# Attention over channels on one core: TensorE's order around the Gram block, VectorE's order of reading T, and the place of element 2's Gram block

## The chip, the core and the metric

The kernel runs on one core of one Trainium2 chip. The metric is the device time in microseconds (us) of one execution. Five engines work beside each other, each through its own list of instructions in order, and wait for each other on semaphores: TensorE (PE) multiplies into the eight PSUM banks, VectorE (DVE) and ScalarE (ACT) read these banks, GpSimd (POOL) works in SBUF alone, and SyncE (SP) issues transfers. TensorE's clock has two levels, 1.2 and 2.4 GHz; the profile gives it as a share of the higher one.

## The reference

Input x has shape (8, 256, 32, 16): batch element b, position s, channel c, and m. For each element:

```python
xn = groupnorm(x, G=8)                      # groups of 2 of the 16 m; over s and c
Q, K, V = (einsum('oc,bscm->bsom', W, xn) + bias for W, bias in (q, k, v))   # 256 outputs each
A = softmax(Q' @ K', axis=-1)               # per (b, m): 256 x 256, summed over s
out = einsum('bmcC,bmsC->bsCm', A, V')
y = x + einsum('oc,bscm->bsom', Wo, out) + bo
```

All is float32.

## The kernel before, in words

The kernel never forms Q and K. For an element and an m it needs only the 32x32 Gram matrix of the centred x (`xc`), its column sums, and the group's variance. T = (normalised Gram) x Wk plus bias terms is a 32x256 matrix for each m, and the scores Q'K' are Wq times T. The 16 m of an element are 4 groups of 4: `t` counts 0 to 3 and `q` the four partition quarters. The work of an element is pipelined over the elements around it, and each element is 16 slots, `s`. In every slot each of three engines does one piece of the scores: PE one 99x512 matmul into one of four score banks (`score`, L449), which is 3 slots ahead; DVE its row maxima (`maximum`, L693), 2 slots ahead; ACT the exponentials with their row sums, two instructions of 256 columns (`exponentials`, L942). `score(n)` waits until ACT has done exponentials n-4.

Between these, every engine has pieces of other elements at fixed slots. The orders are written out by hand: the tables `PE_AT`, `DVE_AT`, `ACT_AT` (L42 to L46) give the slot of each piece for elements 1 to 7, the bodies of `element` in the PE block (L535) and in the DVE block (L746) hold a list of their own for element 0 and the order inside a slot.

The pieces, for an element j of which element b = j-3 or j-2 is in its slots:

- `sum_rows(j)`, `sum_groups(j)`, `mean(j)`, `read_mean(j)`: group means (PE, DVE, PE, DVE); POOL then centres the rows (`centre_rows`, L1008).
- `gram_of(j)` (L379, 64 small matmuls) and `sums_of(j)` (L389, 64 more) write the Gram matrices and column sums; `read_gram(j)` (DVE L659) copies them; POOL takes the diagonal (`diagonal`, L1016); `sum_diagonal(j)` (DVE L663), `variance(j)` (PE L405) and `read_variance(j)` (DVE L668, L675) give the variances.
- POOL's `deviations(j)` (L1030, L1050, L1056) makes the scaled sums `ssum` and `sblk`, and `normalise(j)` (L1024) the scaled Gram `gnorm`.
- `t_product(j)` (PE L431) writes T in four banks: t=0 into `acc` (its upper half), t=1 into `bx`, t=2 into `by`, t=3 into `bz`; `tb_product(j)` (L437) writes the bias rows into `bz`. DVE reads them with `read_t(j, t)` (L682) and `read_tb(j)` (L688). POOL splits T in a high and a low part (`parts`, L1082 and L1084), and SP's transfers stack them for the score matmuls.
- `column_sums(b, g)` (PE L473, 16 matmuls of 256 columns, g = 0 to 3) sums the exponentials, weighted with the inverse row sums (`invert`, DVE L704), into the lower half of `acc`; `read_acc`, `a_columns` (L489), `read_a`, POOL's `scale_wo` (L1095, L1099), `weights` (L507, L515), `read_weights` (DVE L728, L730) make the output weights; `y_half` (PE L531) makes half of y, and ACT (`read_y01`, L954) or DVE (`read_y23`, L741) reads it. From element 2 on ACT reads y01 of element b-2 behind the exponentials of slot 0.

The bank `bx` carries sums, means, Gram matrices and variances of the elements from 2 on, and T's part t=1. So `gram_of(j)` waits until DVE has read t=1 of element j-1 (`pe.wait_ge(t_done, 4 * (j - 1) + 2)`, L375; for j = 2 the wait isn't there, because that block runs before T of element 1 is written). `t_done` counts reads of T in DVE's order. In elements 1 to 4 PE's slot 10 is `score`, `gram_of(b+3)`, `column_sums(b, 0)`; DVE's slot 8 is `maximum`, `read_t(., 0)`, its slot 9 `maximum`, `read_tb`, `read_t(., 1)`.

Before element 0 PE runs `score(0)`, `score(1)`, `gram_of(2)`, `sums_of(2)`, `score(2)` (L629 to L633), and DVE `centre(2)`, `maximum(1)`, `diagonal_first(2)`, `read_gram(2)`, `sum_diagonal(2)` (L902 to L906). `t_product(1)` in slot 0 of element 0 waits for `gram_done` 3, that is for `read_gram(2)`.

## Time and profile before

| | us |
|---|---|
| runs of the kernel before | 188.49, 189.87, 194.72 (median 189.87) |
| the profiled execution | 190.13 |
| its span in the profile | 188.1 |
| busy in the span: PE, DVE, ACT, POOL | 161.7, 133.0, 130.2, 96.9 |

The profile covers the span; 2.0 us of the execution lie around it. Times in rows are counted from the span's start. The first exponentials of an element (slot 0) start at 23.8 us for element 0, 50.6 for element 1, 68.1 for element 2 and 86.8 for element 3. Ends of matmuls are modelled, so that two neighbouring ones seem to overlap a little. A figure in square brackets behind a row is the idle time of the engine before it, and what ended it.

### The profile page before, as it was taken

Reading aid. Unit: us, or ns where it says so; the run is one execution under the profiler, and the core shown is the slowest. Engines: PE = TensorE matmul, PEld = TensorE weight load, DVE = VectorE, ACT = ScalarE, POOL = GpSimd, SP = SyncE. Lnnn points to the kernel's source line nnn. Section 1 sums busy time; section 2 is a strip of 40 time slices with the busy share of each in tenths; the row PEclk is TensorE's granted clock in tenths of the full one; section 3 lists DMA queues with packets and bytes.
Section 4 is the critical chain, followed back from the end, with each engine's and each line's share of the span. In section 5 each row is a group of like instructions: output and inputs, shape, how many; then the busy total and the mean of one; then the engine's idle time right before and its main releaser. Section 6 shows DMA issues by size and latency. Waiting matters only on the chain.

```text
span 188.1 us, 6983 instructions
## 1 busy us (share of the span) xinstructions
PE 161.7 (86%) x2672; PEld 93.6 (50%) x2672; DVE 133.0 (71%) x327; ACT 130.2 (69%) x533; POOL 96.9 (52%) x155
## 2 busy tenths in 40 slices
PE   7986969979799799979997899798989879999872
PEld 7765845524344464446444644463435435344541
DVE  4349359857469887888788777877898684678531
ACT  2001045975378969996998689968999999499721
POOL 1561385985386757675767476757274050007300
PEclk9999765555869999999999999999999995899996
DMA  6613974289289629962883297518935790002032
GB/s 220 179 37 72 228 213 179 39 191 236 112 162 196 213 30 205 226 233 36 186 202 151 29 200 154 201 24 202 227 124 82 195 265 35 0 0 115 2 137 89
DMA packets 10286, 26.46 MB, mean 141 GB/s; under 512 B 2731, under 2 KB 3726, under 8 KB 10254
## 3 DMA queue, kind: packets, MB, share of 16 engines
q1 hardware_dynamic: 8512, 25.16, 52.4%
q10 hardware_dynamic: 1742, 0.87, 1.8%
q8 instruction: 21, 0.34, 0.8%
q14 instruction: 11, 0.09, 0.1%
HBM read 8.85 MB, written 4.19 MB: 69 GB/s over the span
## 4 chain that ended last, share of the span: by engine, by line
PE 54%; ACT 14%; DVE 8%; issue 6%; POOL 3%; DVEq 0%; POOLq 0%
PE s_bank L449 15%; PE acc L473 14%; ACT e_sb L942 11%; PE bz L531 7%; ACT yb L954 3%; PE acc L431 3%; PE bx L379 3%; PE bx L389 2%; PE bz L437 2%; PE by L507 2%; DVE negmax L693 2%; PE bx L405 2%; DVE t_sb L682 1%; DVE t_sb L688 1%; PE by L515 1%
## 5 line engine op out<-in xcount | busy, mean ns | idle before, releaser
L942 ACT ACTIVATE e_sb<-s_bank,negmax 128x256 f32<-128x256 f32 x256 | 117.5, 494 | 25.0 <-DVE negmax L693 24.8
L693 DVE TENSOR_REDUCE negmax<-s_bank 128x2 f32<-128x512 f32 x128 | 84.8, 678 | 13.6 <-PE s_bank L449 13.1
L449 PE MATMUL s_bank<-stack,wq_st 99*128 99x512 f32 x128 | 56.8, 505 | 5.5 <-ACT e_sb L942 5.4
L942 ACT ACTIVATION_READ_ACCUMULATOR e_sb<-s_bank,negmax 128x1 f32 x256 | 57.8, 226 | 0.0
L449 PEld LDWEIGHTS s_bank<-stack,wq_st 99*128 99x128 f32 x128 | 23.3, 208 | 31.8 <-issue 31.5
L473 PE MATMUL acc<-e_sb,recip 128*32 128x256 f32 x512 | 37.6, 415 | 0.6 <-DVE recip L704 0.6
L1095 POOL TENSOR_TENSOR aR<-aT,coef 128x32 f32<-128x32 f32 (+1 forms) x16 | 3.6, 247 | 36.3 <-DVE aT L717 36.3
L1084 POOL TENSOR_TENSOR t_parts<-t_sb,t_parts 128x768 fp32r<-128x768 f32 (+1 forms) x14 | 21.7, 1552 | 1.1
L473 PEld LDWEIGHTS acc<-e_sb,recip 128*32 128x32 f32 x512 | 14.4, 115 | 15.0 <-issue 8.8
L1008 POOL TENSOR_TENSOR xc<-xs,nm 128x512 f32<-128x512 f32 x13 | 13.8, 1080 | 10.1 <-DVE nm L653 10.1
L954 ACT ACTIVATE yb<-bz,beff 128x256 f32<-128x256 f32 x16 | 6.7, 470 | 14.6 <-PE bz L531 14.6
L1030 POOL TENSOR_TENSOR rs_all<-vare,power 128x8 f32<-128x8 f32 x8 | 13.2, 1644 | 4.7 <-DVE vare L668 4.5
L531 PE MATMUL bz<-xT,wf 32*32 32x256 f32 x224 | 15.0, 382 | 0.1
L1099 POOL TENSOR_TENSOR ws<-wo_sb,aR 128x1024 f32<-128x1024 f32 (+1 forms) x8 | 14.4, 1803 | 0.6
L1082 POOL CAST t_parts<-t_sb 128x768 fp32r<-128x768 f32 (+1 forms) x14 | 10.1, 718 | 8.0 <-DVE t_sb L682 8.0
L346 PE MATMUL bz<-idle 128*128 128x128 f32 x60 | 11.3, 351 | 1.0 <-POOL idle L1110 1.0
L379 PE MATMUL bx<-xc 128*32 128x32 f32 x448 | 5.9, 210 | 6.3 <-DVE t_sb L682 4.2
L346 PEld LDWEIGHTS bz<-idle 128*128 128x128 f32 x60 | 9.9, 253 | 2.2 <-issue 1.2
L379 PEld LDWEIGHTS bx<-xc 128*32 128x32 f32 x448 | 5.3, 123 | 8.4 <-issue 8.4
L531 PEld LDWEIGHTS bz<-xT,wf 32*32 32x32 f32 x224 | 5.7, 105 | 6.0 <-issue 2.0
L431 PE MATMUL acc<-wk_sb,gnorm 32*128 32x256 f32 x14 | 5.7, 494 | 3.4 <-issue 2.2
L1016 POOL TENSOR_TENSOR gdiag<-gram,k_sb 128x128 f32<-128x128 f32 x6 | 2.7, 457 | 11.0 <-DVE gram L659 11.0
(119 smaller groups left out, 199.2 us busy)
## 6 DMA issues: line engine op xcount, KB each, us to landing
stack<-t_parts SPq DMA_DIRECT2D x28, 256.0 KB, 5.0
stack<-t_parts SPq DMA_DIRECT2D x36, 128.0 KB, 5.0
xs<-x_rows SPq DMA_DIRECT2D x8, 512.0 KB, 4.9
xT<-x_cols SPq DMA_DIRECT2D x8, 512.0 KB, 5.6
y_cols<-yb SPq DMA_DIRECT2D x7, 512.0 KB, 5.2
stack<-t_parts SPq DMA_DIRECT2D x8, 32.0 KB
stack<-t_parts ACTq DMA_DIRECT2D x4, 64.0 KB, 3.5
stack<-t_parts SPq DMA_DIRECT2D x4, 64.0 KB, 2.7
```

The costliest lines, as they stand in the source:

```text
L346: nc.tensor.matmul(bz[:, 0:P], idle[:, :], idle[:, :], start=True, stop=True)
L379: mm = nc.tensor.matmul(stat_bank(j)[C * q:C * q + C, C * t:C * t + C], xc[:, j % 2, ch, Q * t + q, 0:C], xc[:, j % 2, ch, Q * t + q, 0:C] ...
L449: nc.tensor.matmul(s_bank[q][:, :], wq_st[:, P * h:P * h + P], stack[:, b % 2, q, 2 * tt:2 * tt + 2, :].rearrange("p t n -> p (t n)"), sta ...
L473: mm = nc.tensor.matmul(acc[C * q:C * q + C, 0:CH], recip[:, at:at + C], e_sb[:, 4 * g + q, i, :], start=(g in opens and i == 0), stop=(g ...
L531: mm = nc.tensor.matmul(dst[C * q:C * q + C, S * i:S * i + S], wf[C * q:C * q + C, t, :], xT[C * q:C * q + C, j, t, :], start=True, stop=True)
L693: nc.vector.tensor_reduce(negmax[:, n % NS, :], s_bank[n % NS][:, :].rearrange("p (i n) -> p i n", i=2), op=ALU.max, axis=AX.X, negate=Tru ...
L942: last = nc.scalar.activation(e_sb[:, s, i, :], s_bank[q][:, CH * i:CH * i + CH], ACT.Exp, bias=negmax[:, q, i:i + 1], accum_out=rowsum[:, ...
L954: last = nc.scalar.activation(yb[:, yb_of(j), t, :], src[:, S * i:S * i + S], ACT.Identity, bias=beff[:, t:t + 1])
L1008: last = nc.gpsimd.tensor_tensor(xc[:, j % 2, ch, :, 0:C].rearrange("p (g k) c -> p g k c", g=G), xs[:, j % XS, ch, :, :].rearrange("p (g ...
L1030: nc.gpsimd.tensor_tensor(rs_all[:, :], vare[:, j, 0:8], power[:, :], ALU.pow).then_inc(rs_all_done, 1)
L1084: nc.gpsimd.tensor_tensor(t_parts[:, j % 2, 1, rows, :], t_sb[:, rows, :], t_parts[:, j % 2, 0, rows, :].bitcast(f32), ALU.subtract).then_ ...
L1099: nc.gpsimd.tensor_tensor(ws[:, :, ms, :], wo_sb[:, :, None, :].to_broadcast([P, HC, n, C]), aR[:, :, 0, ms, None].to_broadcast([P, HC, n, ...
```

## The change

On PE, `column_sums(b, 0)` goes ahead of `gram_of(b + 3)` in slot 10 of elements 1 to 4. On DVE, `read_t(b + 2, 1)` goes from slot 9 to slot 8, ahead of `maximum` and `read_tb` of slot 9; in element 0 it goes ahead of `read_tb` too. `gram_of(2)` and `sums_of(2)` go from before `score(2)` to slots 2 and 3 of element 0, and their reads on DVE to slots 3 and 4; `gram_of(2)` gets the wait for t=1 of element 1, and `t_product(1)` waits for the mean of element 2 in place of its Gram. Everything that follows in element 0 moves to later slots (variance of 2 from slot 3 to 5, T of 2 from 9 to 10, `gram_of(3)` from 12 to 13, `sums_of(3)` from 13 to 14; DVE's `read_gram(3)` from 13 to 15), and `variance(3)` and what is tied to it goes into element 1, whose `sum_rows(4)` and `mean(4)` move one slot. The instructions are the same ones, and so is the number of each. The half of y that DVE reads (`read_y23`) is not touched by the diff.

```diff
--- before.py
+++ after.py
@@ -41,7 +41,7 @@
 
 PE_AT = dict(sums2=1, rows=1, mean=3, sums3=3, y23=4, a=5, t=7, gram=10, sums0=10, gsums=12, weights=13, sums1=13,
              variance=15, y01=15)
-DVE_AT = dict(variance=0, invert3=1, groups=2, mean=4, acc=4, y23=5, invert0=6, a=6, t0=8, tb=9, t1=9, t2=10, t3=11,
+DVE_AT = dict(variance=0, invert3=1, groups=2, mean=4, acc=4, y23=5, invert0=6, a=6, t0=8, t1=8, tb=9, t2=10, t3=11,
               invert1=11, gram=13, weights=14, invert2=13, trace=14)
 ACT_AT = dict(y01=0)
 
@@ -370,7 +370,7 @@
                 pe.wait_ge(centred, j + 1)
                 if j == 0:
                     pe.wait_ge(centred_by_dve, 1)
-                if j >= 3:
+                if j >= 2:
 
                     pe.wait_ge(t_done, 4 * (j - 1) + 2)
                 for t in range(T):
@@ -397,9 +397,6 @@
                 pe.wait_ge(trace_done, j + 1)
                 if j == 0:
                     pe.wait_ge(set_blocks, 2)
-                if j == 2:
-
-                    pe.wait_ge(t_done, 4 + 2)
 
                 for k in range(2):
                     mm = nc.tensor.matmul(stat_bank(j)[:, T * k:T * (k + 1)], half_m[:, k, :], trace[:, :],
@@ -417,7 +414,7 @@
                 pe.wait_ge(gnorm_done, j + 1)
                 if j == 1:
 
-                    pe.wait_ge(gram_done, 3)
+                    pe.wait_ge(mean_done, 3)
                     pe.wait_ge(tb_done, 1)
                 elif j >= 2:
 
@@ -542,30 +539,36 @@
                         if s == 0:
                             t_product(1)
                             tb_product(1)
+                        if s == 2:
+                            gram_of(2)
                         if s == 3:
+                            sums_of(2)
+                        if s == 5:
                             variance(2)
-                        if s == 5:
+                        if s == 7:
                             sum_rows(3)
-                        if s == 7:
+                        if s == 8:
                             mean(3)
-                        if s == 9:
+                        if s == 10:
                             t_product(2)
                             tb_product(2)
-                        if s == 11:
+                        if s == 12:
                             column_sums(0, 0)
-                        if s == 12:
+                        if s == 13:
                             gram_of(3)
-                        if s == 13:
+                        if s == 14:
                             column_sums(0, 1)
                             sums_of(3)
-                        if s == 15:
-                            variance(3)
                         continue
+
+                    late = 1 if b == 1 else 0
+                    if b == 1 and s == 1:
+                        variance(3)
                     if s == PE_AT["sums2"]:
                         column_sums(b - 1, 2)
-                    if b + 3 < B and s == PE_AT["rows"]:
+                    if b + 3 < B and s == PE_AT["rows"] + late:
                         sum_rows(b + 3)
-                    if b + 3 < B and s == PE_AT["mean"]:
+                    if b + 3 < B and s == PE_AT["mean"] + late:
                         mean(b + 3)
                     if s == PE_AT["sums3"]:
                         column_sums(b - 1, 3)
@@ -576,10 +579,10 @@
                     if b + 2 < B and s == PE_AT["t"]:
                         t_product(b + 2)
                         tb_product(b + 2)
+                    if s == (6 if last else PE_AT["sums0"]):
+                        column_sums(b, 0)
                     if b + 3 < B and s == PE_AT["gram"]:
                         gram_of(b + 3)
-                    if s == (6 if last else PE_AT["sums0"]):
-                        column_sums(b, 0)
                     if b + 3 < B and s == PE_AT["gsums"]:
                         sums_of(b + 3)
                     if s == (9 if last else PE_AT["sums1"]):
@@ -628,8 +631,6 @@
             pe.wait_ge(t_done, 4)
             score(0)
             score(1)
-            gram_of(2)
-            sums_of(2)
             score(2)
             for b in range(B):
                 element(b)
@@ -753,43 +754,47 @@
                         if s == 0:
                             read_t(1, 0)
                         if s == 1:
+                            read_t(1, 1)
                             read_tb(1)
-                            read_t(1, 1)
                         if s == 2:
                             read_t(1, 2)
                         if s == 3:
                             read_t(1, 3)
+                            diagonal_first(2)
                         if s == 4:
+                            read_gram(2)
+                            sum_diagonal(2)
+                        if s == 6:
                             read_variance(2)
-                        if s == 6:
+                        if s == 7:
                             sum_groups(3)
-                        if s == 7:
+                        if s == 9:
                             read_mean(3)
-                        if s == 9:
                             invert(0, 0)
-                        if s == 10:
+                        if s == 11:
                             read_t(2, 0)
-                            read_tb(2)
-                        if s == 11:
                             read_t(2, 1)
                         if s == 12:
-                            read_t(2, 2)
+                            read_tb(2)
                             invert(0, 1)
                         if s == 13:
+                            read_t(2, 2)
+                        if s == 14:
                             read_t(2, 3)
-                            read_gram(3)
-                        if s == 14:
                             invert(0, 2)
                         if s == 15:
-                            sum_diagonal(3)
+                            read_gram(3)
                         continue
-                    if b + 2 < B and s == DVE_AT["variance"]:
+                    late = 1 if b == 1 else 0
+                    if b == 1 and s == 0:
+                        sum_diagonal(3)
+                    if b + 2 < B and s == DVE_AT["variance"] + late:
                         read_variance(b + 2)
                     if s == DVE_AT["invert3"]:
                         invert(b - 1, 3)
-                    if b + 3 < B and s == DVE_AT["groups"]:
+                    if b + 3 < B and s == DVE_AT["groups"] + late:
                         sum_groups(b + 3)
-                    if b + 3 < B and s == DVE_AT["mean"]:
+                    if b + 3 < B and s == DVE_AT["mean"] + late:
                         read_mean(b + 3)
                     if s == DVE_AT["acc"]:
                         read_acc(b - 1)
@@ -802,10 +807,10 @@
                     if b + 2 < B:
                         if s == DVE_AT["t0"]:
                             read_t(b + 2, 0)
+                        if s == DVE_AT["t1"]:
+                            read_t(b + 2, 1)
                         if s == DVE_AT["tb"]:
                             read_tb(b + 2)
-                        if s == DVE_AT["t1"]:
-                            read_t(b + 2, 1)
                         if s == DVE_AT["t2"]:
                             read_t(b + 2, 2)
                         if s == DVE_AT["t3"]:
@@ -901,9 +906,6 @@
             dve.wait_ge(xs_loaded[2], 16)
             centre(2, (0, 1), centred)
             maximum(1)
-            diagonal_first(2)
-            read_gram(2)
-            sum_diagonal(2)
             dve.wait_ge(w_loaded, 16 * 4)
             nc.vector.tensor_reduce(wv_sum[:, :], wv_sb[:, :, :], op=ALU.add, axis=AX.X).then_inc(wv_sum_done, 1)
             for b in range(B):
```

## Rows read from the trace of the kernel before

**Rows 1.** The longest waits over the span, and PE's at the Gram block (us, times, longest).

```profile
ACT e_sb L942 <- DVE negmax L693: 24.8, 22, 8.3
...
ACT yb L954 <- PE bz L531: 14.6, 8, 2.7
...
PE bx L379 <- DVE t_sb L682: 4.2, 4, 1.1
```

**Rows 2.** The page: TensorE's granted clock in 40 slices, and the chain by engine.

```profile
PEclk9999765555869999999999999999999995899996
...
PE 54%; ACT 14%; DVE 8%; issue 6%; POOL 3%; DVEq 0%; POOLq 0%
```

**Rows 3.** Windows of elements 1, 2 and 5: busy us of each engine, clock, DMA.

```profile
50.60:68.07 17.47, 15.14 (x255) 8.36 (x259) 14.30 (x35) 15.19 (x64) 13.09 (x20) 0.90 0.66 154
68.07:86.75 18.68, 16.66 (x328) 9.55 (x321) 15.37 (x37) 15.87 (x68) 12.69 (x20) 1.00 0.72 175
...
124.50:141.00 16.50, 14.31 (x174) 7.23 (x170) 13.24 (x32) 14.27 (x61) 9.84 (x16) 1.00 0.68 164
```

**Rows 4.** Timeline of element 2, slots 8 to 11 (start us, us, engine, line, operation).

```profile
79.64 0.47 DVE L682 SCALAR_TENSOR_TENSOR t_sb<-bk_sb,ssum,acc 128x256 f32<-128x256 f32 x1
...
79.93 1.02 PE L449 MATMUL s_bank<-stack,wq_st 99*128 99x512 f32 x3
...
80.47 0.69 DVE L693 TENSOR_REDUCE negmax<-s_bank 128x2 f32<-128x512 f32 x1 [0.36 <-PE s_bank L449]
...
81.08 0.46 DVE L688 SCALAR_TENSOR_TENSOR t_sb<-bk_sb,rows_all,bz 32x256 f32<-32x256 f32 x1
...
81.47 0.46 DVE L682 SCALAR_TENSOR_TENSOR t_sb<-bk_sb,ssum,bx 128x256 f32<-128x256 f32 x1
...
82.07 0.75 PE L379 MATMUL bx<-xc 128*32 128x32 f32 x64 [1.13 <-DVE t_sb L682]
...
82.68 1.07 PE L473 MATMUL acc<-e_sb,recip 128*32 128x256 f32 x16
```

**Rows 5.** Timeline of element 2, its end: weights read, y01 read.

```profile
87.25 0.29 DVE L728 TENSOR_TENSOR wf<-by,k_sb 128x128 f32<-128x128 f32 x1 [0.88 <-PE by L515]
...
89.66 0.84 ACT L954 ACTIVATE yb<-bz,beff 128x256 f32<-128x256 f32 x2 [1.87 <-PE bz L531]
```

**Rows 6.** Timeline of element 5, which has no Gram block.

```profile
137.39 1.07 PE L473 MATMUL acc<-e_sb,recip 128*32 128x256 f32 x16
...
139.07 0.47 ACT L942 ACTIVATE e_sb<-s_bank,negmax 128x256 f32<-128x256 f32 x1 [0.35 <-DVE negmax L693]
...
140.24 0.47 PE L449 MATMUL s_bank<-stack,wq_st 99*128 99x512 f32 x1 [0.90 <-ACT e_sb L942]
```

**Rows 7.** Timeline of the start: Gram block of element 2, T of element 1.

```profile
25.27 1.08 PE L379 MATMUL bx<-xc 128*32 128x32 f32 x64 [1.97 <-DVE xc L834]
...
26.11 1.04 PE L389 MATMUL bx<-xc 128*32 128x1 f32 x64
...
28.08 0.24 POOL L1056 TENSOR_TENSOR sblk<-ssum,k_sb 128x32 f32<-128x32 f32 x1
...
29.70 1.06 PE L437 MATMUL bz<-wk_sb,sblk 128*32 128x256 f32 x2
...
30.69 1.65 PE L449 MATMUL s_bank<-stack,wq_st 99*128 99x512 f32 x3
```

**Rows 8.** Timeline of element 0 from its slot 9 on.

```profile
39.72 0.79 PE L431 MATMUL acc<-wk_sb,gnorm 32*128 32x256 f32 x1 [1.22 <-POOL gnorm L1024]
...
43.03 1.94 PE L473 MATMUL acc<-e_sb,recip 128*32 128x256 f32 x16
...
49.68 0.30 DVE L659 COPY gram<-bx 128x132 f32<-128x132 f32 x1 [2.88 <-PE bx L389]
...
50.61 0.47 ACT L942 ACTIVATE e_sb<-s_bank,negmax 128x256 f32<-128x256 f32 x1 [3.14 <-DVE negmax L693]
...
51.58 0.58 PE L405 MATMUL bx<-trace,half_m 128*128 128x4 f32 x4 [1.30 <-DVE trace L663]
```

## The prediction, made before the changed kernel was built or run

> **What bounds the kernel now.** I read the waits first. ACT is idle for 24.8 us behind DVE's maxima and for 14.6 us behind the y01 matmuls, and PE is idle for 4.2 us, in 4 pieces of up to 1.1 us, ahead of a Gram block, each time until DVE has read a piece of T [rows 1]. An idle engine costs only if the end hangs on it, so the chain comes next: 54% of it is PE, 14% ACT, 8% DVE [rows 2]. Then the windows: in element 2 (18.68 us) PE is busy for 16.66 us, ACT for 15.87, DVE for 15.37, POOL for 12.69; element 5, which has no Gram block, takes 16.50 [rows 3]. So no engine is full, and PE's order of work sets the pace. The loop closes at y01: PE comes to the end of its slots, y01 follows, ACT has waited for it (1.87 us in element 2) and only then does the next exponentials, which PE's next scores need [rows 5]. Whatever PE's order saves between two y01 is saved in full, as long as DVE and ACT keep up.
>
> **The steady part, elements 1 to 4.** In element 2, PE's three scores of slots 8 to 10 end at 79.93 + 1.02 = 80.95. Then it waits 1.13 us for T's part t=1, whose read begins at 81.47, behind a maximum (80.47) and the bias rows (81.08); the Gram block starts at 82.07, the column sums of group 0 at 82.68, and these take 1.07 us [rows 4]. After the change, the column sums start at 80.95. What they wait for is there: T's part in acc was read from 79.64 on, and the inverse row sums are of slot 6. They end near 82.0. DVE reads t=1 straight behind t=0, from 80.05 to 80.5, in the 0.36 us which it sat idle ahead of the maximum [rows 4]. That maximum slips by at most 0.05 us, as the score it reads ends at about 80.45. So the Gram block finds its bank free and starts near 82.0, and the slot-11 scores start about 1.0 us earlier. Each half of this edit alone would hide nearly all of the wait; the two don't add up.
>
> Can the others follow? DVE's bias rows stay at 81.1 and the maximum of slot 10 comes 0.4 us earlier, since t=1 no longer stands ahead of it. From there to the copy of the Gram matrices DVE has little idle time, so it is 0.3 to 0.4 us earlier there and not 1.0. But it then waits for the weight matmuls anyway, 0.88 us ahead of the copy at 87.25 [rows 5]; with PE 1.0 us earlier and DVE 0.35 us earlier that wait is 0.2 us, and y01 still gains nearly the whole. For ACT: the exponentials of slot 12 start 0.35 us earlier and then run back to back, 0.9 us a slot, so that the last score that PE issues in the element (slot 15) needs exponentials that are done about a microsecond before it. POOL gets the bias rows and t=1 0.4 us earlier. What stands behind the moved column sums on PE is the Gram block alone, and it isn't later than before. The sum for elements 1 to 4 is the wait that goes, 4.2 us [rows 1], less 0.05 us each: 4.0 us. Its bounds are 1.0 us (the wait returns as one for ACT, rival C) and 4.4.
>
> **Element 5** has the new order on DVE but no Gram block. There PE waits 0.90 us for ACT at 140.24, because the exponentials of slot 12 began at 139.07, 0.35 us after ACT ran out, behind the bias rows, t=1 and a maximum [rows 6]. With t=1 moved into an idle gap that maximum is 0.4 us earlier: 0.35 us saved, bounds 0 and 0.5. Elements 6 and 7 read no T, so nothing changes there.
>
> **Element 0 and the seam to element 1.** This is the part that I know least. The steps, with PE at its lower clock:
>
> - Before, PE did the Gram block and sums of element 2 from 25.27 to 27.15, ahead of score 2. T of element 1 stood behind them and the copy of the Gram, its bias rows started at 29.70, the next scores at 30.69; POOL's sblk, which the bias rows need, ended at 28.08 + 0.24 = 28.3 [rows 7]. After, T doesn't wait for the Gram copy and runs near 24.3, but the bias rows still wait for POOL until 28.4. So the scores start at 29.4 in place of 30.69: 1.3 us gained, not 4, and the idle time of PE grows, which before held 1.9 us of Gram and sums.
> - These two blocks now stand in slots 2 and 3: 1.08 us [rows 7] and about 0.85, minus 1.9 us. Behind them DVE's diagonal waits for the sums until about 33.4, with a maximum queued behind it: ACT gets its seventh exponentials (slot 6) at about 34.4, as before. PE then waits about 0.9 us for the trace ahead of variance 2: minus 0.9 us.
> - Before, PE waited 1.22 us at 39.72 for POOL's gnorm of element 2 [rows 8]. POOL has that ready at 39.7 again: it splits T of element 1 about 1.5 us earlier but then waits for the later variance. PE arrives at about 40.6, so the wait is used up: plus 1.2 us.
> - Before, ACT lost 3.14 us at 50.61, because DVE stood 2.88 us in the copy of Gram 3 at 49.68, with two maxima behind it, and PE lost 1.30 us at 51.58 to the trace of element 3 [rows 8]. With the copy in slot 15 behind two more maxima and variance 3 in the next element, both mostly go: plus 1.3 us on PE.
>
> The sum is 1.3 - 1.9 - 0.9 + 1.2 + 1.3 = 1.0 us. Moving rows and mean of element 4 by a slot I cost at nothing: centring it took place well ahead of the Gram block, and POOL idles. By ACT alone the gain would be more (3.14 us less some 1.5 that comes back two slots later). I take 1.2 us, nearer PE's sum since PE is the chain. The bounds: minus 2.0 (the 1.9 us of added blocks with nothing regained) and plus 3.0 (ACT's wait gone whole).
>
> **The sum.** 4.0 + 0.35 + 1.2 = 5.55 us. The profiled execution took 190.13 us (span 188.1 and 2.0 around it), 0.3 above the median of the runs, 189.87. 190.13 - 5.55 = 184.6; against the median it is 184.3. I take 184.8, as two of the three terms were laid out by hand from one execution, and such schedules leave out small waits. A difference of under 2%, 3.8 us, is about what can't be told from none; that border is at 186.1.
>
> **The rivals.**
>
> B, only the steady part pays. Element 0 costs up to 2.0 us instead of giving 1.2: 190.1 - 4.35 + 2.0 = 187.8. For it: 3 us of PE idle time at the start are not filled by anything, and DVE has a new wait at slot 3. Against it: the stalls of 3.14 and 1.30 us at its end are plain in the trace.
>
> C, the wait at the Gram block turns into one for ACT. Element 5 has the coming order already, column sums right behind the scores, and there PE waits 0.90 us for exponentials [rows 6]. If that came back in elements 1 to 4, only 0.2 us each would be left: 190.1 - 0.8 - 0.35 - 1.2 = 187.8; with nothing from the start, 189. Against it: in element 5 neither the Gram block nor the sums stand ahead of that score (0.75 us [rows 4] and about as much), and in elements 1 to 4 they do.
>
> D, slower: the clock. It stands at half in the slices from 28 to 47 us and not fully up until 56 [rows 2]. Element 1 still has 0.90 of it [rows 3]. Full activity near 43 to 50 us, the column sums and Gram 3, came before it rose. After the change PE idles longer at the start and its dense part may come later. If the clock stays at the lower level through element 1, the price is: 4 column sums at 1.94 for 1.07 us, 3.5 [rows 8, 4]; 16 scores, (1.65 - 1.02)/3 = 0.21 each, 3.4 [rows 7, 4]; Gram and sums 0.7; 7.6 us, of which a fifth is paid already: 6.1. With the start's gain lost (1.2) it is 184.8 + 7.3 = 192.1, and with a third of element 2 as well, 194.3. It decides at the first column sums of element 1: if they take 1.9 us and those after them too, it is slower. Against it: the amount of PE work is the same, and the last of element 0 is as dense as it was.
>
> The Trainium skill, "TensorE: Matmul & The Clock Gate", Part 1, says that the throttled state is the default and that activity releases the throttle. It speaks for D, since the change takes activity out of the start; by it the clock could be lower there, where the rows show it at the lower level already, so the trace has nothing for it to take until about 47 us.
>
> E, the same thing the other way: with fewer stalls from 47 us on, the clock doesn't fall again near 52 us. Column sums there, of 1.94 us as the row at 43.03 [rows 8], become 1.07, the sum rows and scores shorter too: 1.5 to 2.5 us more, 182.7.
>
> **How the numbers follow.** The forecast has 0.56, and of it 0.03 above 186.1; E 0.11, B 0.16, C 0.10, D 0.07. Faster by over 2%: 0.53 + 0.11 = 0.64. Within 2%: 0.03 + 0.16 + 0.10 = 0.29. Slower: 0.07. The range has to reach E and B and may leave out D and the end of C: 182.0 to 188.2.
>
> **What would show it.** Right: PE's wait ahead of the Gram block is gone from the waits in elements 1 to 4, the column sums of group 0 follow the scores at once, and the windows from y01 to y01 are about 17.7 us in elements 2 to 4; the first exponentials of element 1 come near 47.5 instead of 50.61 and those of element 2 about 2 us earlier than 68.1. Wrong: a wait of the slot-13 scores for ACT in elements 1 to 4 (C); element 2's first exponentials at 68 us or later (B, D); clock digits of 5 behind 48 us (D). A wait of DVE for sums_of(2) of more than 2 us would also break the sum of element 0.

## The result, and the profile after

The changed kernel took 183.31 us (median of 4 runs, 182.40 to 183.57) against 189.52 for the one before; the ratio is 0.968, 95% interval 0.962 to 0.974. The forecast was 184.8 us, range 182.0 to 188.2. The profiled execution took 182.40 us (span 180.3) against 190.13. Here and below, a ratio with an interval is taken over the runs within 1.5% of the fastest of the same kernel, and a median over all its runs.

The clock in 40 slices and the chain by engine, from the page after; these answer to [rows 2]:

```profile
PEclk9996995555969999999999999999999999999996
...
PE 63%; ACT 21%; issue 6%; DVE 6%; POOL 2%; POOLq 0%; DVEq 0%
```

More of the chain is on PE and ACT than before (63% and 21%, from 54% and 14%). PE does the same 2672 matmuls in both. Its busy time fell from 161.7 to 158.0 us, and its idle time (span less busy) from 26.4 to 22.3: of the 7.8 us of span, 4.1 are waiting that went, and 3.7 are the same matmuls in less time, with 26.7 us at the lower clock in place of 40.3 (how that is worked out stands with the experiments). From the 13th slice to the 39th the digits are all 9s. Before there was a 5 and an 8 about where element 6 ends and element 7 begins, and the window of that stretch in the trace of the kernel before shows what it was (columns as in [rows 3]):

```profile
151.00:162.30 11.30, 10.09 (x106) 5.00 (x106) 7.21 (x17) 8.58 (x39) 2.37 (x3) 0.70 0.38 113
```

A granted clock of 0.70, in a stretch that no edit touches. This has to be kept apart from the change in all that follows.

The waits after, which answer to [rows 1]:

```profile
ACT e_sb L944 <- DVE negmax L694: 17.8, 15, 6.8
...
ACT yb L956 <- PE bz L528: 12.5, 8, 3.2
...
PE bz L434 <- POOL sblk L1058: 2.6, 1, 2.6
```

PE's wait ahead of the Gram block, 4.2 us in 4 pieces, is not among the waits any more. ACT waits 17.8 us for maxima in place of 24.8, and 12.5 for y01 in place of 14.6. There is a new one: 2.6 us for POOL's `sblk`, once, in the start.

Element 2 in the timeline after, where [rows 4] stood before:

```profile
78.24 0.47 DVE L683 SCALAR_TENSOR_TENSOR t_sb<-bk_sb,ssum,acc 128x256 f32<-128x256 f32 x1
...
78.53 1.02 PE L446 MATMUL s_bank<-stack,wq_st 99*128 99x512 f32 x3
...
78.63 0.48 DVE L683 SCALAR_TENSOR_TENSOR t_sb<-bk_sb,ssum,bx 128x256 f32<-128x256 f32 x1
...
79.07 0.69 DVE L694 TENSOR_REDUCE negmax<-s_bank 128x2 f32<-128x512 f32 x1
...
79.47 1.07 PE L470 MATMUL acc<-e_sb,recip 128*32 128x256 f32 x16
...
79.67 0.46 DVE L689 SCALAR_TENSOR_TENSOR t_sb<-bk_sb,rows_all,bz 32x256 f32<-32x256 f32 x1
...
80.36 0.77 PE L379 MATMUL bx<-xc 128*32 128x32 f32 x64
```

The scores end at 79.55. The column sums follow at 79.47 (ends are modelled), the read of t=1 (78.63) stands behind t=0, the Gram block begins at 80.36. From the three scores' start to the Gram block it was 2.14 us and is 1.83, with the column sums already done; those began 2.75 us behind that start before and begin 0.94 behind it now. Windows from the first exponentials of one element to those of the next (elements 1 to 5, answering to [rows 3]):

```profile
46.21:65.32 19.11, 17.25 (x313) 9.31 (x314) 15.00 (x37) 15.33 (x64) 14.52 (x22) 0.91 0.64 148
...
65.32:84.63 19.31, 17.89 (x368) 10.80 (x367) 15.21 (x37) 15.84 (x69) 12.68 (x20) 1.00 0.69 169
84.63:102.43 17.80, 16.56 (x294) 9.58 (x298) 15.20 (x37) 15.84 (x69) 12.67 (x20) 1.00 0.66 153
102.43:120.39 17.96, 17.07 (x359) 10.14 (x348) 15.20 (x37) 15.85 (x69) 12.70 (x20) 1.00 0.64 152
120.39:137.50 17.11, 15.30 (x180) 7.72 (x180) 14.97 (x37) 15.69 (x68) 11.21 (x18) 1.00 0.69 159
```

By these windows elements 1 and 2 are longer than before (19.11 for 17.47 us and 19.31 for 18.68): ACT reaches them earlier and then waits. So the y01 reads, which close the loop, are the better marks. From one to the next it took, before and after: 18.69 and 17.82 us (y01 of element 0 to that of element 1), 19.33 and 17.95, 18.82 and 17.47, 16.32 and 15.92, then 18.13 and 15.82, and 13.15 in both. So the 7.7 us between the two profiled executions are made up of 1.4 us up to the first y01 (70.97 to 69.55), 0.87 + 1.38 + 1.35 = 3.60 in elements 2 to 4, 0.40 in element 5, and 2.31 in element 6, which holds the stretch at a clock of 0.70 that no edit touches.

The start in the timeline after, which answers to [rows 7, 8]:

```profile
24.51 0.50 PE L446 MATMUL s_bank<-stack,wq_st 99*128 99x512 f32 x1 [1.04 <-DMA stack<-t_parts]
...
24.94 0.48 PE L428 MATMUL acc<-wk_sb,gnorm 32*128 32x256 f32 x1
...
28.23 1.06 PE L434 MATMUL bz<-wk_sb,sblk 128*32 128x256 f32 x2 [2.57 <-POOL sblk L1058]
...
34.19 0.47 ACT L944 ACTIVATE e_sb<-s_bank,negmax 128x256 f32<-128x256 f32 x1 [1.41 <-DVE negmax L694]
...
40.31 0.79 PE L428 MATMUL acc<-wk_sb,gnorm 32*128 32x256 f32 x1
...
46.21 0.47 ACT L944 ACTIVATE e_sb<-s_bank,negmax 128x256 f32<-128x256 f32 x1
...
48.51 0.29 PE L389 MATMUL bx<-xc 128*32 128x1 f32 x11 [0.48 <-issue]
...
48.84 0.30 DVE L660 COPY gram<-bx 128x132 f32<-128x132 f32 x1 [1.54 <-PE bx L389]
...
50.00 0.47 ACT L944 ACTIVATE e_sb<-s_bank,negmax 128x256 f32<-128x256 f32 x1 [1.65 <-DVE negmax L694]
...
50.30 0.58 PE L402 MATMUL bx<-trace,half_m 128*128 128x4 f32 x4 [0.60 <-DVE trace L664]
```

PE waits 1.04 us for a transfer of the stack ahead of score 2, which now has no Gram block in front of it. T of element 1 runs at 24.94, then PE waits 2.57 us for `sblk` and does the bias rows at 28.23, 1.5 us earlier than before. The seventh exponentials come at 34.19 after a wait of ACT for DVE, T of element 2 at 40.31 with no wait for `gnorm`. The first exponentials of element 1 are at 46.21 in place of 50.61. DVE's wait of 2.88 us at the copy of Gram 3 is 1.54 now, ACT's of 3.14 at the start of element 1 has become one of 1.65 two slots later (50.00), and PE's trace wait of 1.30 is 0.60. But of 4.4 us at the first exponentials of element 1, 2.75 are left at those of element 2 (65.32 for 68.07) and 1.42 at the first y01:

```profile
65.77 0.41 PE L470 MATMUL acc<-e_sb,recip 128*32 128x256 f32 x3 [1.00 <-issue]
...
69.55 0.84 ACT L956 ACTIVATE yb<-bz,beff 128x256 f32<-128x256 f32 x2 [3.20 <-PE bz L528]
```

Here PE stands for 1.00 us in the middle of column sums, with nothing in the profile that it waits for, and ACT waits 3.20 us for y01. PE's own work shows where the rest went. The sums of element 3 were done at 49.61 before (the first row below) and at 48.80 now, 0.8 us earlier and not 4.4. Up to the first y01 PE does 1036 matmuls in both traces, but of these 307 stood behind the first exponentials of element 1 before, and 389 do now. Its idle time up to the first y01 was 9.66 us and is 8.91. A wait of 0.82 us that went belongs to element 1's own Gram block (the second row) and so to the order and not to the start. From the trace before:

```profile
48.87 0.74 PE L389 MATMUL bx<-xc 128*32 128x1 f32 x64
...
63.40 0.76 PE L379 MATMUL bx<-xc 128*32 128x32 f32 x64 [0.82 <-DVE t_sb L682]
```

### The profile page after: what moved, and what is told of

Read it like the earlier page. It is cut to its first block, busy times and chain, and to the rows that moved or that the text cites. A ratio compares the mean times of both kernels' runs of the same rounds, so it can differ in the third digit from the quotient of the medians.

```text
span 180.3 us, 6983 instructions
## 1 busy us (share of the span) xinstructions
PE 158.0 (88%) x2672; PEld 91.6 (51%) x2672; DVE 132.3 (73%) x327; ACT 130.1 (72%) x533; POOL 96.7 (54%) x155
## 4 chain that ended last, share of the span: by engine, by line
PE 63%; ACT 21%; issue 6%; DVE 6%; POOL 2%; POOLq 0%; DVEq 0%
ACT e_sb L944 17%; PE s_bank L446 16%; PE acc L470 13%; PE bz L528 7%; PE bz L346 4%; ACT yb L956 3%; PE bx L402 2%; PE bx L379 2%; PE bz L434 2%; PE bx L389 2%; PE bx L356 2%; PE acc L428 2%; PE by L504 2%; DVE negmax L694 1%; PE bx L364 1%
## 5 line engine op out<-in xcount | busy, mean ns | idle before, releaser
L944 ACT ACTIVATE e_sb<-s_bank,negmax 128x256 f32<-128x256 f32 x256 | 117.5, 495 | 18.2 <-DVE negmax L694 17.8
L446 PE MATMUL s_bank<-stack,wq_st 99*128 99x512 f32 x128 | 55.8, 491 | 6.5 <-ACT e_sb L944 5.4
L446 PEld LDWEIGHTS s_bank<-stack,wq_st 99*128 99x128 f32 x128 | 22.8, 201 | 31.8 <-issue 29.7
L470 PE MATMUL acc<-e_sb,recip 128*32 128x256 f32 x512 | 35.8, 393 | 1.6 <-issue 1.0
L470 PEld LDWEIGHTS acc<-e_sb,recip 128*32 128x32 f32 x512 | 13.7, 111 | 16.0 <-issue 9.3
L1010 POOL TENSOR_TENSOR xc<-xs,nm 128x512 f32<-128x512 f32 x13 | 13.8, 1080 | 11.3 <-DVE nm L654 11.3
L956 ACT ACTIVATE yb<-bz,beff 128x256 f32<-128x256 f32 x16 | 6.7, 470 | 12.5 <-PE bz L528 12.5
L346 PE MATMUL bz<-idle 128*128 128x128 f32 x60 | 10.8, 337 | 1.0 <-POOL idle L1112 1.0
L346 PEld LDWEIGHTS bz<-idle 128*128 128x128 f32 x60 | 9.3, 237 | 2.6 <-issue 1.6
L434 PE MATMUL bz<-wk_sb,sblk 128*32 128x256 f32 x14 | 5.2, 461 | 2.6 <-POOL sblk L1058 2.6
L710 DVE COPY a_sb<-acc 128x256 f32<-128x256 f32 x9 | 3.8, 425 | 4.2 <-PE acc L470 4.1
L705 DVE RECIPROCAL recip<-rowsum 128x8 f32<-128x8 f32 x32 | 6.2, 194 | 0.9 <-ACT e_sb L944 0.7
L428 PE MATMUL acc<-wk_sb,gnorm 32*128 32x256 f32 x14 | 5.2, 456 | 1.7 <-issue 1.7
```

Of the source, the lines that this page charges most:

```text
L346: nc.tensor.matmul(bz[:, 0:P], idle[:, :], idle[:, :], start=True, stop=True)
L446: nc.tensor.matmul(s_bank[q][:, :], wq_st[:, P * h:P * h + P], stack[:, b % 2, q, 2 * tt:2 * tt + 2, :].rearrange("p t n -> p (t n)"), sta ...
L470: mm = nc.tensor.matmul(acc[C * q:C * q + C, 0:CH], recip[:, at:at + C], e_sb[:, 4 * g + q, i, :], start=(g in opens and i == 0), stop=(g ...
L944: last = nc.scalar.activation(e_sb[:, s, i, :], s_bank[q][:, CH * i:CH * i + CH], ACT.Exp, bias=negmax[:, q, i:i + 1], accum_out=rowsum[:, ...
L956: last = nc.scalar.activation(yb[:, yb_of(j), t, :], src[:, S * i:S * i + S], ACT.Identity, bias=beff[:, t:t + 1])
L1010: last = nc.gpsimd.tensor_tensor(xc[:, j % 2, ch, :, 0:C].rearrange("p (g k) c -> p g k c", g=G), xs[:, j % XS, ch, :, :].rearrange("p (g ...
```

## The experiments

The twelve experiments below time eight kernels, some of them more than once, in three sets beside the kernel before. Times scattered there much more than in the first result: the kernel before took between 186.67 and 201.97 us in 34 runs. Each run also gives its mean granted clock, and most of the scatter goes with it. Time at the lower clock is worked out as 2 x (1 - mean clock) x span, since the lower level is half of the higher one. A least-squares fit over the 107 runs with a known clock, with a constant of its own for each kernel and one slope for all, gives 0.343 us of time (standard error 0.012) for each us at the lower clock, and takes the scatter within a kernel from 3.2 us to 1.0. "At equal clock" means below: by this fit. At 30 us at the lower clock the kernels stand at:

| kernel | runs | us at 30 us of lower clock (standard error) |
|---|---|---|
| before | 35 | 188.3 (0.2) |
| changed | 16 | 183.6 (0.3) |
| PE's order alone | 4 | 185.1 (0.5) |
| DVE's order alone | 4 | 183.6 (0.5) |
| both orders, old start | 18 | 184.0 (0.3) |
| new start, old orders | 6 | 188.1 (0.4) |
| changed, with POOL's edit | 12 | 182.2 (0.3) |
| both orders, old start, with POOL's edit | 6 | 182.7 (0.4) |
| changed, with filler | 6 | 186.1 (0.4) |

How far to trust the table: a constant of its own for each set moves no difference to the kernel before by more than 0.3 us. The fit over the 38 runs within 1.5% of the fastest of their kernel has a slope of 0.27 (error 0.06) and moves these differences by at most 0.5 us, but for the filler kernel, which it puts 0.6 us above the changed one and not 2.4.

The Trainium skill, "TensorE: Matmul & The Clock Gate", Terms, puts the cost of the throttled time at that time multiplied by 1 - K/N, which is 0.5 at half clock. Here it is 0.343, and the measurement decides. The price also differs by place, by two comparisons below: 0.18 in element 0 and 0.37 in element 1.

**pe_only**, on the kernel before:

```diff
+                    if s == (6 if last else PE_AT["sums0"]):
+                        column_sums(b, 0)
                     if b + 3 < B and s == PE_AT["gram"]:
                         gram_of(b + 3)
-                    if s == (6 if last else PE_AT["sums0"]):
-                        column_sums(b, 0)
```

> The kernel before with one edit: column sums of group 0 ahead of the Gram block in slot 10 of elements 1 to 4. Theory (the two orders are two ways around one wait): the column sums, 1.07 us, fill the wait of 1.13 us, so nearly all goes: PE's wait ahead of the Gram block falls from 4.2 us to under 0.5 in total, 4.0 us saved, ratio 0.979. Element 5 gains nothing. Rival (each order gives half): about 2 us, ratio 0.99. Rival (the wait turns into one for ScalarE): under 1 us, and PE's scores wait for the exponentials in slot 13.

Medians of 187.95 us for 194.21, ratio 0.982 (0.942 to 1.021), too wide to say anything by itself; at equal clock 3.2 us less than before. The wait ahead of the Gram block has gone from the list of waits. Element 2 in its timeline:

```profile
83.37 1.07 PE L473 MATMUL acc<-e_sb,recip 128*32 128x256 f32 x16
...
83.96 0.46 DVE L682 SCALAR_TENSOR_TENSOR t_sb<-bk_sb,ssum,bx 128x256 f32<-128x256 f32 x1
...
84.35 0.67 DVE L693 TENSOR_REDUCE negmax<-s_bank 128x2 f32<-128x512 f32 x1
...
84.57 0.75 PE L379 MATMUL bx<-xc 128*32 128x32 f32 x64
```

The column sums end at 84.44 and the read of t=1 at 84.42, so the Gram block starts 0.1 us behind the sums. The y01 reads of elements 2 to 4 lie 18.08, 18.23 and 17.86 us apart, 2.67 us less in sum than before; element 5 gives nothing (16.33 for 16.32). That is the theory, somewhat short in size (about 3.2 of the 4.0 us expected fall to these three elements, by their waits of 1.13, 1.13 and 1.12 us); neither rival.

**dve_only**, on the kernel before:

```diff
-DVE_AT = dict(..., tb=9, t1=9, ...)
+DVE_AT = dict(..., t1=8, tb=9, ...)
+                        if s == DVE_AT["t1"]:
+                            read_t(b + 2, 1)
                         if s == DVE_AT["tb"]:
                             read_tb(b + 2)
-                        if s == DVE_AT["t1"]:
-                            read_t(b + 2, 1)
```

> The kernel before with the other edit alone: VectorE reads t=1 of T behind t=0, ahead of the maximum and the bias rows, in elements 1 to 5. Theory: the read ends before the scores of slot 10 do, so the Gram block starts at once: 4.1 us saved in elements 1 to 4 and 0.35 in element 5, 4.4 in all, ratio 0.977. Rival (each order gives half): 2 us, ratio 0.99.

185.97 us for 194.21, ratio 0.969 (0.940 to 0.999); at equal clock 4.7 us less than before. y01 to y01 17.51, 17.88 and 17.50, so 3.95 us less in three elements, and 15.96 in element 5, 0.36 less. Element 2:

```profile
83.31 0.47 DVE L682 SCALAR_TENSOR_TENSOR t_sb<-bk_sb,ssum,bx 128x256 f32<-128x256 f32 x1
...
84.15 0.76 PE L379 MATMUL bx<-xc 128*32 128x32 f32 x64
...
84.75 0.67 DVE L693 TENSOR_REDUCE negmax<-s_bank 128x2 f32<-128x512 f32 x1
...
84.77 1.07 PE L473 MATMUL acc<-e_sb,recip 128*32 128x256 f32 x16
```

t=1 is read by 83.78, before the scores end at 84.2, and the Gram block follows them at once. The second maximum starts 1.54 us behind the three scores' start (83.21), where in pe_only it starts 1.93 behind it (82.42). This edit alone does all that the two do.

**orders_only**, both of the diffs above.

> The kernel before with both orders and without the move of element 2's Gram block. Theory: the two don't add up, 4.4 us saved, ratio 0.977, within 0.5 us of each alone. Rival (they add up): 8 us, ratio 0.957. What the whole change has over this one is then the worth of the start: the measured ratio is 0.968, so the start would be worth 1.5 to 2 us.

189.60 us for 194.21, with 49.6 us at the lower clock (median of its runs) against 47.3; at equal clock 4.3 us less than before. y01 to y01 17.71, 17.96, 17.47, 15.92. The two orders don't add up: 3.2, 4.7 and 4.3 us for one, the other and both, with errors of 0.5, 0.5 and 0.3 us.

**start_only**, the changed kernel with both diffs above undone.

> The changed kernel with both orders of elements 1 to 5 put back as they were: only the start (Gram block of element 2 in slots 2 and 3, all of element 0 that follows from it, variance 3 in element 1). Theory (the start has a worth of its own, by PE's sum 1.2 us): ratio 0.990 to 0.994, PE waits of 1.1 us ahead of the Gram blocks in elements 1 to 4 are back, first exponentials of element 1 near 46 to 47 us in place of 50.6. Rival (the start only shifts, and the gain beyond 4.4 us came from the clock in the last elements): ratio 0.998 to 1.002, with the first y01 at 71 us as before.

189.83 us for 194.21, ratio 0.985 (0.966 to 1.004). The PE wait ahead of the Gram blocks is back:

```profile
PE bx L379 <- DVE t_sb L683: 4.3, 4, 1.1
```

Its first exponentials of element 1 are 22.9 us behind those of element 0, as in the changed kernel (22.5; before 26.8). But it then took 25.3 us to the first y01, where the kernel before took 20.4, with one stop of PE of 1.33 us and a clock of 0.88 for 0.92. At equal clock it is only 0.2 us (error 0.5) faster than before. Its median time at the lower clock was 32 us against 47 for the kernel before and 50 for the two orders. So a second theory came up: the start pays through the clock. The profiles spoke for it too: with the old start, the clock stayed down through element 1 in all three profiles of this set. Both orders, slices of 4.7 us:

```profile
PEclk9999555556965559999999999999999996999997
```

**after_again** and **orders_again**, the two kernels once more on one chip.

> The changed kernel once more, unchanged, for the time that it spends at TensorE's lower clock. In the traces so far the stretch at the lower clock went on through most of element 1 (from about 50 to 66 us) in three of the four kernels with the old start (not in the profiled execution of the kernel before) and in neither of the two with the new start. Theory (the new start mainly shortens the time at the lower clock): median of that time near 27 to 35 us, against 45 to 50 for the kernels with the old start on the same chip, and the first exponentials of element 2 less than 43 us behind the first of element 0. Rival (chance): its time at the lower clock spreads as widely as theirs, and the medians are within 5 us.

> Both orders without the move of element 2's Gram block, once more, beside the changed kernel on one chip. A least-squares line through the runs so far gives 0.35 us of time per us at the lower clock, and at equal time at the lower clock this kernel is as fast as the changed one (183.6 and 184.1). Theory (the start pays by the clock): median 3 to 5 us above the changed kernel's, with 10 to 15 us more at the lower clock; equal when that is accounted for. Rival (the start pays by its own schedule, 1.2 us by the prediction): 1 to 2 us above it, with the same time at the lower clock.

186.04 and 186.49 us (ratios to before 0.972, 0.961 to 0.984, and 0.967, 0.950 to 0.983), with medians of 37.2 and 38.0 us at the lower clock. The difference that the theory asked for, 3 to 5 us, isn't there.

**after_third** and **orders_third**, again.

> The changed kernel a third time, beside the kernel with both orders alone. So far, at equal time at the lower clock, the start is worth 0.3 us, and it is open whether it also shortens that time: it did between the first two sets of runs (27 against 50 us) and not in the second (37 against 38). Theory (it does): median time at the lower clock at least 8 us under that of the kernel with the orders alone, and a median time 3 us lower. Rival (no effect but chance): within 4 us of it, and times within 1.5 us.

> Both orders without the move of the Gram block, the other side of the comparison. Theory (the start shortens the time at the lower clock): 40 to 50 us at the lower clock, 187 to 190 us. Rival: as the changed kernel, within 1.5 us.

185.16 and 185.08 us (ratios 0.974, 0.959 to 0.989, and 0.983, 0.974 to 0.993), with 33.4 and 32.9 us at the lower clock. The second theory fell: side by side, the start changes neither the time nor the clock measurably. The profile of the changed kernel in this set shows the clock down in element 1 with the new start as well, and it took 22.92 us from the first exponentials of element 1 to those of element 2, against 19.11 in the first profile:

```profile
PEclk9999695556955599999999999999999966999995
```

Of these windows 13.8 us were at the lower clock against 3.4, so 10.4 us more of it cost 3.8 us.

The profile of orders_third also tells where the start's gain is lost, with the clock nearly alike. With the old start element 0 took 26.27 us from its first exponentials to those of element 1 (20.5 us of it at the lower clock), and from there to the first y01 it took 20.16 (3.2). With the new start, in the first profile, it is 22.53 (17.1) and 23.34 (3.3). So 3.7 us are gained ahead of the seam, and 3.2 are given back behind it.

**after_pool** and **after_pool_again**, on the changed kernel:

```diff
+            inverse_all(0)
+            coefficients(0)
             diagonal(1)
             normalise(1)
-            inverse_all(0)
-            coefficients(0)
             deviations(1)
```

> The changed kernel with one edit on GpSimd: element 0's inverse deviations and coefficients are made in its idle time ahead of element 1's diagonal, not between that and element 1's sums. That takes about 2.9 us off the way to sblk of element 1, for which TensorE's bias rows wait from 25.7 to 28.2 us. Theory: sblk ends near 25.4, TensorE's wait of 2.57 us goes, element 0's next scores start 2.6 us earlier, and the end is 1.5 to 2.6 us earlier, ratio to the changed kernel 0.986 to 0.992. Rival (something else is late next, the stack's transfers or VectorE's centring): under 0.5 us.

> The changed kernel with GpSimd's edit, again, on one chip with the changed kernel. In the last set it was at 182.6 us, 1.0 to 1.5 us better at equal time at the lower clock. Theory: again 1 to 2 us better than the changed kernel at equal time at the lower clock, ratio 0.985 to 0.995 of the medians if their time at the lower clock is alike. Rival (chance): no better than it.

182.63 us against 186.04 for the changed kernel in the second set, 181.40 against 185.16 in the third (ratios to before 0.959, 0.946 to 0.973, and 0.960, 0.946 to 0.973). At equal clock it is 1.4 us faster (error 0.4). T of element 1, `sblk` and the bias rows in its timeline:

```profile
24.70 0.48 PE L428 MATMUL acc<-wk_sb,gnorm 32*128 32x256 f32 x1
...
25.54 0.24 POOL L1058 TENSOR_TENSOR sblk<-ssum,k_sb 128x32 f32<-128x32 f32 x1
...
25.84 0.62 PE L434 MATMUL bz<-wk_sb,sblk 128*32 128x256 f32 x2 [0.42 <-POOL sblk L1058]
```

The wait of 2.57 us is 0.42. In the changed kernel, between 22 and 25 us, POOL had made element 0's coefficients, which nobody needs before `scale_wo`, while it had sat idle for 3.1 us just before. Its runs also had less time at the lower clock (medians 29.6 and 26.2 us against 37.2 and 33.4). Here too a gain shrinks behind the seam: element 0 takes 19.39 us for 22.53, and up to the first y01 it is 44.10 for 45.87. It has the lowest medians of all.

**orders_pool**, the same diff with both orders and the old start.

> Both orders and GpSimd's coefficients of element 0 in its idle time, without the move of the Gram block. Here T of element 1 waits for the copy of the Gram matrices, which waits for GpSimd's sums until 28.0 us; with these 2.9 us earlier the copy is bound by the Gram block itself (27.2 us), so T can start near 27.6 in place of 28.5 and its bias rows at 28.8 in place of 29.7. Theory: about 0.9 us better than the two orders alone, and 1 to 2 us behind the changed kernel with the same edit, since only there TensorE can use all that GpSimd gains. Rival (the start move is worth nothing here either): equal to it.

183.33 us (ratio to before 0.973, 0.960 to 0.986) against 181.40 for the version above; at equal clock 182.7 against 182.2, a difference within its error. At equal clock it is 1.3 us better than the two orders alone, where 0.9 was expected. So the start's place beside POOL's edit is worth 0.5 us (error 0.5) at equal clock. The other 1.4 us of the medians go with less time at the lower clock (26.2 against 33.1 us), and whether that belongs to the start is not settled by one set.

**after_fill**, on the changed kernel. `fill` multiplies zeros into columns 256 to 383 of `by`, which nothing else uses:

```diff
                             t_product(1)
+                            fill(14)
                             tb_product(1)
```

> The changed kernel with 14 matmuls on zeros (128x128) between T of element 1 and its bias rows, where TensorE sat idle for 2.57 us; their result is read by nobody. Theory (TensorE's clock falls after this idle stretch, and element 0 is long for that): the granted clock stays at its upper level past 28 us in the profile, the time at the lower clock falls to under 15 us, and with 0.35 us saved per us of it the kernel is 3 to 5 us faster than the changed one. Rival (the low density of element 0's work, not this one gap, lets the clock fall): it falls a few us later, and the gain is under 1.5 us.

186.35 us (ratio to before 0.960, 0.942 to 0.978) against 186.04 for the changed kernel: no gain. The filler covers the gap, and the bias rows still wait for `sblk` (28 records, two for each matmul):

```profile
24.70 3.39 PE L351 MATMUL by<-idle 128*128 128x128 f32 x28
...
28.74 0.62 PE L439 MATMUL bz<-wk_sb,sblk 128*32 128x256 f32 x2 [0.64 <-POOL sblk L1064]
```

The clock stayed up until about 34 us in place of 27, then it fell all the same, and again in element 1:

```profile
PEclk9998799755855599999999999999999966999995
```

One run with only 15.7 us at the lower clock took 180.09 us; the others scattered as those of the other kernels. The lower-clock time that it saves lies in element 0, where it is cheap: from the first exponentials of element 0 to those of element 1 it took 21.39 us against 22.53, 1.14 us less for 6.4 us less at the lower clock (10.7 against 17.1). At equal clock the fit puts this kernel 2.4 us above the changed one, but, as said under the table, that size is not firm. The rival said a fall of the clock a few us later and a gain under 1.5 us, and both came. Its reason, the low density of element 0's work, was not tested by itself.

## Why the prediction was right, and where it wasn't

- **Steady part, 4.0 us.** Right. In elements 2 to 4 PE waited 1.13, 1.13 and 1.12 us before, which less 0.05 each makes 3.2; the first profiles gave 3.60. Of it 0.17 us is a stop of PE with no releaser that was longer before (0.47 us at 104.09, against 0.30 at 100.41). The fourth wait, 0.82 us, was element 1's. At equal clock both orders give 4.3 us (error 0.3) for elements 1 to 5, forecast 4.35.
- "Each half of this edit alone would hide nearly all of the wait; the two don't add up." Right, shown by pe_only, dve_only and orders_only. PE's order alone falls short (2.67 us against 3.95 in three elements): t=1 is still read behind the bias rows, and the maximum behind it is 0.4 us later than with DVE's order.
- **Element 5, 0.35 us.** Measured 0.40, and 0.36 with DVE's order alone; 0 with PE's order alone.
- **The start, 1.2 us.** Too large: start_only gives 0.2 us (error 0.5), and the changed kernel against both orders 0.35 (error 0.4). The steps were mostly there: the scores at 29.22 (laid out: 29.4), PE's trace wait ahead of variance 2 0.40 us (0.9), seventh exponentials at 34.19 (34.4), T of element 2 at 40.31 (40.6), first exponentials of element 1 at 46.21 (47.5), and ACT's wait "that comes back two slots later" 1.65 (1.5). The step that failed is the last, that PE's 1.3 us would stay saved across the seam. 4.4 us at the first exponentials of element 1 shrank to 1.4 at the first y01, of which 0.8 is element 1's new order, and up to there the changed kernel also had 24 us at the lower clock against 31. ACT got ahead, but PE, which had been the chain all along, was only 0.8 us ahead at the sums of element 3 and had 389 matmuls left for 307. I had laid PE out only to the first column sums of element 1. Two of the losses, stops of PE of 0.48 us at 48.51 and 1.00 at 65.77, were in no row that I had. These counts place the rest of the loss, but no run splits it into causes.
- **The sum.** At equal clock the whole change gives 4.6 us (error 0.3), forecast 5.55; the difference is the start. The first result gives 6.2. The changed kernel's four runs there had 26 to 28 us at the lower clock and the profiled one before had 40; the clock of the other runs before is not on record. By the fit, then, about 1.6 of the 6.2 us are the clock. So it was luck in part that the total came this close: the start gave 0.9 us less than its term, and the clock more than made up for it.
- **Rivals.** C fell: no wait of the slot-13 scores for ACT took the old one's place (5.4 us of such waits in all, before and after). B was right that only the steady part pays, but the start costs nothing instead of 2.0. D's mechanism is real, but it doesn't come from this change: the clock was down in element 1 in profiles of either start, and cost 3.8 us there (22.92 for 19.11), where 6.1 was priced. (D's 194.3 should be about 194.6 by its own price, a third of 7.6 us on top of 192.1; nothing hangs on it.) E didn't come: the clock fell in the changed kernel too, from 51 to 55 us.

## What to carry to other kernels

Where a block waits for one buffer of several, read that buffer first; here that alone gave 4.7 us, at least as much as moving other work into the wait (3.2), and doing both paid once (4.3). A gain at one point of the timeline is worth what is left of it at the next point where the loop closes: here the first y01, not the first exponentials of the next element. And before two kernels are compared, compare their time at the lower clock: here it moved the same program by about 13 us (39 us more at the lower clock, at 0.343 each).

## What was not expected of the hardware

- The same program spent between 28 and 66 us at TensorE's lower clock from run to run, and its times went with it, from 186.67 to 201.97 us.
- PE stops in the middle of a block of like matmuls, with nothing in the profile that it waits for, and at the same instructions from kernel to kernel. In 11 of the 14 profiles it stops in `sums_of(3)`, with the last 11 (new start) or 10 (old start) records still to come, for 0.37 to 2.84 us; in 13 of the 14 in `sums_of(6)`, with 15 to come, for 0.17 to 0.85; and in four of the seven with the new start ahead of the last records of a block of column sums, for 0.17 to 1.33 us (1.00 at 65.77 in the first). The longest, in after_pool_again:

```profile
47.48 0.38 PE L389 MATMUL bx<-xc 128*32 128x1 f32 x11 [2.84 <-issue]
```

The filler kernel tells what fixes the place. It has 28 more matmul records ahead of `sums_of(6)`, and there PE stops with 43 records to come in place of 15, which is 28 earlier:

```profile
103.18 0.54 PE L394 MATMUL bx<-xc 128*32 128x1 f32 x43 [0.38 <-issue]
```

That speaks for a place that goes by a count of PE's instructions, and not by the time or the work (in `sums_of(3)` the filler kernel has no stop). The profiles also have DMA packets of the kind "instruction" (0.02 MB each) near it. In after_pool_again one moved between 45 and 46 us, inside the stop. In the first profile of the changed kernel one moved between 46 and 47 us, ahead of the stop that ended at 48.51, and one between 63 and 64, ahead of the one that ended at 65.77. That PE waits for such a packet fits, but no run tried it.
